# Who adds the constants row to the attention layers' rows: VectorE (DVE) or GpSimd (POOL)

## The reference, cut to what matters

```python
def _gat_layer(x, src, dst, ea, W, We, a_s, a_d, a_e, b, g, beta):
    h = x @ W
    ...
    alpha = jax.nn.leaky_relu(alpha, NEG_SLOPE)
    alpha = _segment_softmax(alpha, dst, N)
    out = jax.ops.segment_sum(h[src] * alpha[:, None], dst, num_segments=N) + b
    mu = out.mean(-1, keepdims=True)
    var = ((out - mu) ** 2).mean(-1, keepdims=True)
    return (out - mu) * jax.lax.rsqrt(var + LN_EPS) * g + beta
```

## Time and profile before

| | |
|---|---|
| median of 3 runs | 6403.81 us (6377.07 to 6413.65) |
| span of the profiled execution | 5398.9 us |
| median less this span | 1004.9 us |
| DVE busy over the span | 3792.3 us (70%) |
| ACT busy over the span | 3176.1 us (59%) |
| POOL busy over the span | 2893.9 us (54%) |
| first and last `out` of pass d0 | 1120.1 and 1277.0 us |
| first and last `out` of pass d1 | 1632.2 and 1788.8 us |
| first and last `out` of pass d2 | 2145.3 and 2300.9 us |

### The profile page before, as it was taken

How to read it: one execution, slowest core, us unless ns; L and a number is a source line. 1 busy time by engine, 2 the same in 40 slices (tenths; PEclk the granted TensorE clock), 3 DMA queues, 4 the chain that set the end, 5 groups by cost and what they waited for, 6 DMA issues and landing times. The chain is left out here.

```text
span 5398.9 us, 104328 instructions
## 1 busy us (share of the span) xinstructions
PE 3821.1 (71%) x23663; PEld 3143.4 (58%) x23663; DVE 3792.3 (70%) x10843; ACT 3176.1 (59%) x11279; POOL 2893.9 (54%) x2759
## 2 busy tenths in 40 slices
PE   6355889566747685768575768678688787977775
PEld 5354778565537453645474545456577676866665
DVE  2575889688849784978596767677567675756666
ACT  2022889577848684868482323356577685655554
POOL 0466766603650463066205867676376564757776
PEclk8698999888979797979676767677799998988777
DMA  8898999556955694578463446555489797872221
GB/s 183 129 301 269 383 362 278 176 148 179 283 175 149 203 283 154 156 229 278 149 184 126 131 129 189 167 158 177 165 282 303 248 305 238 246 189 66 62 66 57
DMA packets 918273, 1074.23 MB, mean 199 GB/s; under 512 B 202780, under 2 KB 565066, under 8 KB 917107
## 3 DMA queue, kind: packets, MB, share of 16 engines
q1 hardware_dynamic: 763570, 890.24, 50.5%
q0 software_dynamic: 90944, 180.06, 13.6%
q10 hardware_dynamic: 63556, 1.81, 1.6%
HBM read 509.54 MB, written 566.14 MB: 199 GB/s over the span
## 5 line engine op out<-in xcount | busy, mean ns | idle before, releaser
L2358 POOL DMA_INDIRECT H<-gat_rows,src_i x784 | 804.1, 1026 | 1032.9 <-POOLq L79 620.9
L1909 POOL DMA_INDIRECT s_G<-sage_rows,src_i x588 | 602.4, 1025 | 369.6 <-issue 161.0
L1695 POOL DMA_INDIRECT r_G<-rel_rows,idx x392 | 441.7, 1127 | 216.8 <-issue 110.2
L1708 PE MATMUL r_t<-r_oh,relv 8*128 8x512 f32 x294 | 227.4, 862 | 217.5 <-issue 77.2
L2547 PE MATMUL p_M<-Wg,p_hT 128*128 128x132 f32 x2352 | 336.6, 287 | 63.1 <-DVE p_res L2604 48.8
L1743 ACT ACTIVATE r_mT<-r_t 128x512 f32<-128x512 f32 x147 | 87.4, 594 | 460.4 <-PE r_t L1711 460.1
L2547 PEld LDWEIGHTS p_M<-Wg,p_hT 128*128 128x128 f32 x2352 | 290.3, 192 | 113.0 <-issue 96.0
L2604 DVE SCALAR_TENSOR_TENSOR p_res<-p_M,p_rr,cg 128x132 f32<-128x132 f32 x1176 | 333.8, 346 | 2.5 <-PE p_M L2547 1.4
L1304 PE MATMUL d_S<-ones,d_sqT 128*128 128x1 f32 x1568 | 224.3, 264 | 144.0 <-DVE d_ve L1449 144.0
L2686 PEld LDWEIGHTS p_pl_p<-Wn,p_pl_h 128*128 128x128 f32 x1568 | 205.9, 198 | 201.8 <-ACT p_pl_h L2780 154.9
L2686 PE MATMUL p_pl_p<-Wn,p_pl_h 128*128 128x128 f32 x1568 | 225.3, 289 | 132.6 <-ACT p_pl_h L2780 132.4
(11 more groups left out here) (482 smaller groups left out, 12286.0 us busy)
## 6 DMA issues: line engine op xcount, KB each, us to landing
gat_rows<-p_res SPq DMA_DIRECT2D x294, 264.0 KB
sage_rows<-p_pl_s SPq DMA_DIRECT2D x294, 256.0 KB
gat_rows<-x_row SPq DMA_DIRECT2D x98, 536.0 KB
gat_rows<-d_res SPq DMA_DIRECT2D x147, 264.0 KB
d_hs<-gat_rows SPq DMA_DIRECT2D x147, 256.0 KB
s_hT<-sage_slots_t SPq DMA_DIRECT2D x147, 256.0 KB
slot_rows<-H SPq DMA_DIRECT2D x49, 544.0 KB, 11.5
x_x<-in_x SPq DMA_DIRECT2D x98, 256.0 KB
```

What stands on the lines that cost most here:

```text
L1695: pool.indirect_dma_start(self.G[:, g % 4, k, :], None, table, bass.IndirectOffsetOnAxis(index[:, c:c + 1], 0), bounds_check=bound, oob_is ...
L1708: pe.matmul(pt[:, :], kn.relv[:, l, :], self.oh[:, b.m % self.Y, :], start=True, stop=False)
L1909: pool.indirect_dma_start(self.G[:, g % 4, k, :], None, kn.st[self.l], bass.IndirectOffsetOnAxis(kn.idx[:, c:c + 1], 0), bounds_check=boun ...
L2358: pool.indirect_dma_start(kn.H[:, c, 0:width], None, table, bass.IndirectOffsetOnAxis(index[:, c:c + 1], 0), bounds_check=bound, oob_is_er ...
```

## The change

In the passes d0, d1 and d2, the step `out` goes from DVE's list to a list of its own on POOL. It is the same one instruction of 128x528 on the same operands, with the same wait (`rsc`, raised by `scaled`) and the same signal (`om`). ACT, PE and SP keep their lists.

```diff
@@ -1288,6 +1288,15 @@
+            @block.gpsimd
+            def _(pool):
+                def out(b):
+                    done(pool, rsc, b)
+                    pool.tensor_tensor(res[:, b.s4], res[:, b.s4], spread(self.cg[:, l + 1, :], KT), ALU.add).then_inc(om, 1)
+
+                if not end:
+                    times(pool, [(out, 7)], KG)
+
...
-                def out(b):
-                    done(v, rsc, b)
-                    v.tensor_tensor(res[:, b.s4], res[:, b.s4], spread(self.cg[:, l + 1, :], KT), ALU.add).then_inc(om, 1)
-
...
-                    times(v, once + [(out, 7), (run_sums, 3), (scale, 6), (weigh, 1), (variance, 5)], KG)
+                    times(v, once + [(run_sums, 3), (scale, 6), (weigh, 1), (variance, 5)], KG)
```

## The result

The changed kernel took 6327.35 us (median of 4 runs, 6315.62 to 6340.84), the kernel before 6396.47 us in the same comparison. The ratio is 0.9883, with a 95% interval of 0.9861 to 0.9906. Two more comparisons of the same two kernels gave 0.9913 (0.9878 to 0.9948) and 0.9882 (0.9863 to 0.9902). So the change is worth 0.9 to 1.2%, where 0.7% was forecast, and the time lies 5 us under the range.

What follows compares the result with a forecast made beforehand. The ring of DVE and ACT was taken as the 3.31 us round; at 2.91, 16.0 less 0.6 and 1 gives 14.4 us a pass, 43 in three: 6361 us, range 6332 to 6405 (8 in 10).

Steps and rivals of the forecast that it cites:

- The ring of `scale`, `scaled`, `out` and scan: In d0 to d2, DVE and ACT steps waiting on each other in turn; starts sum to 3.25 us, the round.
- ACT's own list: ACT's steps in a round of d0 to d2, without the wait before `scaled`: 2.91 us, the new pace.
- POOL's addition: The 128x528 addition moved to POOL, once a round: 1.2 us, range 0.7 to 2.34, hidden behind ACT.
- One sign: In the middle of d0 to d2, DVE idle by 0.4 us or more a round, waiting for `deviation`.
- The first rival, exclusion: POOL's addition and DVE's `weigh` cannot run together; most of the gain lost, 6380 to 6410 us, chance 0.24.
- T: Time of POOL's addition, taken as 1.2 us; under exclusion it costs from 1.6 and cancels the gain at 2.0.
- The sum of T + 1.3: Least round under exclusion, from the addition, `weigh`, `variance` and the hand-over to `deviation`: 2.5 us at T = 1.2.
- The steady rounds: Some 40 rounds a pass at the steady pace, each falling from 3.31 to 2.91 us: 16.0 us gained.
- the end of a pass: The last `out` before the barrier: 0.71 us on DVE, 1.2 and a hand-over on POOL, 0.6 us more.
- ramps: The rest of a pass's 49 rounds, outside the 40 steady ones; no gain was counted for them.
- The stores, 1 us a pass: Stores in d0 to d2 that land late now and then and hold `scaled`: 1 us of gain lost a pass.
- 1004.9 us that lie around the span, untouched: Time taken to lie outside the profiled span of 5398.9 us, added unchanged to 5356 for the forecast of 6361.

Runs made afterwards that it cites:

- the second profile of before: The kernel before, unchanged, timed against itself and profiled again: ratio 0.9992 (0.9971 to 1.0013), span 6398.3 us.
- the kernel with two: The changed kernel plus a second POOL addition of the same size behind the first, into a tile nobody reads: ratio 0.9975 (0.9946 to 1.0004).
- the last `own` kernel: The changed kernel with the copy of the heads on POOL and one of four `own` instructions on DVE, behind `weigh`: ratio 0.9881 (0.9861 to 0.9900).

## Why the prediction was wrong in its size and right in its mechanism

- *What bounds the kernel.* Right. The ring of `scale`, `scaled`, `out` and scan was the round, and cutting it made ACT's own list the pace. The forecast was 2.91 us a round; the runs have 2.91 with the addition and without it, and 2.81 when 0.10 is taken from ACT's list.
- *POOL's addition.* Taken as 1.2, measured 1.31 us; hidden, as said. One sign did not come: DVE was to be idle by 0.4 us or more a round. It shows no idle time, since the 0.54 us for which `weigh` is held count as busy.
- *The first rival, exclusion.* The mechanism is true, and so is its condition: at T = 1.31, under 1.6, it costs nothing in a steady round. The sum of T + 1.3 as the round's floor was not borne out: two additions of 1.31 and 1.19 us would give 3.8, and the round was 3.17, since the first lay under the scan. It had a chance of 0.24 for most of the gain being lost; it took none.
- *The steady rounds.* 40 x 0.40 = 16.0 us a pass. In the second profile of before against after the difference of a round is 3.32 - 2.91 = 0.41: right.
- *The step that failed: the end of a pass, "0.6 us more", with every round outside the 40 put down as "ramps", worth nothing.* The cost it names was paid (the last addition takes 1.29 us in place of 0.71), but the gains there were left out. The ring through `out` bound the last rounds as well, and in before PE's clock fell among them, behind PE's waits. The last four distances became 3.4 us shorter, and what follows them 0.1 shorter, not 0.6 longer. The mean of the three passes fell by 19.0 us: 14.5 in the middle, where 16.0 - 1 was forecast, 3.4 + 0.1 at the end, where -0.6 was, and 1.1 less 0.1 at the start, where nothing was; that last part varies by as much from one profile to the next. Three passes: 57 us, not 43.
- *The stores, 1 us a pass.* The middle lost that much, 1.0 us a pass against rounds of 2.91 throughout, but in part by luck. It was nothing in d0. In d1 a `scaled` waited 1.05 us for a store. In d2 it was 1.9 us, around a stretch in which PE's granted clock was 0.50 (from 2763 to 2769 us), which the prediction had no term for. At the start of d1 there is one more wait for a store, of 1.71 us.
- *"1004.9 us that lie around the span, untouched".* Wrong as a statement. The profiled execution was itself a quick one. The three passes were alike in it, so it did not change the sum.
- *The range.* 57 us off the prediction's own 6403.8 give 6347, inside the range. The result lies 19 us below that and 5 below the edge: 7 of the 19 are the median of before, which came to 6396.5 in the comparison, and 12 are not located.

## What to carry to other kernels

When an instruction leaves a ring of two engines, the round falls to the longest single list, and that can be added up from the distances between starts on each engine; do the same sum for the last rounds of a pass, where the ring may bind more than the lists, and look at the granted clock there. Before work goes to POOL, look at which DVE instructions will run beside it: here those with two operands in SBUF, and a one-operand scaling too, were held by a POOL instruction that reads, so lay POOL's work beside a scan or a PSUM reader, or keep DVE some slack. An engine that then shows as full may only be held.

## What the hardware showed that I had not expected

- POOL's addition and DVE's two-operand instructions hold each other by order of arrival: POOL first, DVE's 340 ns became up to 882, 956 and 1156; DVE first by 0.04 us, POOL's addition grew to 1587 ns at the median, from 1157 for the same addition in the kernel with two, while DVE's kept its 708. An instruction of DVE that starts 0.02 us ahead of POOL's got through in 317 ns.
- Short waits of PE were followed by a fall of its granted clock from 1.00 to 0.50, and the fall cost more than the waits: a stall of 1.7 us became some 6 us in d1 of the last `own` kernel, and every d0 to d2 of before ran its last products at 1.98 to 2.11 us in place of 1.15.
- On ACT, when it never waits, an instruction's duration is no measure of its cost. `own` x4 shows 1.57 us in after and 1.28 before, single instructions about 700 ns and 402, but the distance between starts is 0.29 us in both; the same is seen with no work on POOL.
- One and the same kernel had spans of 5398.9 and 6398.3 us in two profiles. The passes that gather and store by DMA were quicker in the first and the compute-bound ones equal; the cause is open.
